# Loading block (0,1) of the adjacency matrix transposed at the start, holding it in four load buffers, and multiplying it in layer 0 in phase 1

## The reference

```python
# layer 0
adj_hat = adj + eye(N)
d = 1 / sqrt(sum(adj_hat, axis=1))
out = (adj_hat * d[:, None] * d[None, :]) @ (X @ W) + b
x = layernorm(x + relu(out))
# layer 1
support = x @ weight
output = relu(support + adj @ support + x @ self_weight)
x = layernorm(x + pair_norm(output))
```

## Time and profile before

| | |
|---|---|
| median of 3 runs | 1894.67 us (1894.28 to 1895.56) |
| profiled execution, its own time | 1894.09 us |
| its span in the trace | 1892.2 us |
| mean granted TensorE clock | 0.97 of full speed |
| TensorE, VectorE, ScalarE busy | 92%, 79%, 64% of the span |
| loaded | 566.49 MB from HBM, mean 302 GB/s |

### The profile page before, as it was taken

The page is one execution under the profiler, slowest core; times in us unless marked ns, Lnnn a source line. Parts: engine busy times, 40 slices in busy tenths (PEclk is TensorE's granted clock), DMA queues, the critical chain, the costliest instruction groups (busy, mean ns, idle before and its releaser), DMA issues.

```text
span 1892.2 us, 20585 instructions
## 1 busy us (share of the span) xinstructions
PE 1749.3 (92%) x7682; PEld 1416.7 (75%) x7682; DVE 1491.5 (79%) x1993; ACT 1208.4 (64%) x1648; POOL 21.5 (1%) x34
## 2 busy tenths in 40 slices
PE   2879998987999999989999999999989999999983
PEld 1657886866887888767788888888868888877862
DVE  4889788777878689986767575665589999999987
ACT  4576685785856646655555454454468888888865
POOL 0000000000000000100000000000000000000001
PEclk8999999999999999999999999999999999999995
DMA  9999999899998586954444455545589999999933
GB/s 397 421 422 421 417 399 421 332 397 402 374 384 362 199 355 280 352 181 154 160 174 178 178 178 189 189 176 186 194 322 386 386 386 386 386 376 369 384 149 89
DMA packets 80291, 572.03 MB, mean 302 GB/s; under 512 B 8960, under 2 KB 8960, under 8 KB 12096
## 3 DMA queue, kind: packets, MB, share of 16 engines
q1 hardware_dynamic: 76608, 557.88, 74.9%
q0 software_dynamic: 3584, 12.85, 2.2%
HBM read 566.49 MB, written 4.19 MB: 302 GB/s over the span
## 4 chain that ended last, share of the span: by engine, by line
PE 74%; DVE 15%; DMA 5%; ACT 4%; issue 2%; SPq 0%; POOL 0%; ACTq 0%; DVEq 0%
PE acc L1048 18%; PE acc L1050 18%; PE acc L1054 18%; PE pC L1030 4%; PE pD L1030 4%; DVE raw_low L731 4%; DMA s<-in_adjN 2%; DMA raw<-in_adjT 2%; DVE s L737 2%; ACT hi L557 1%; DVE o_low L731 1%; DVE zr_low L731 1%; DVE ux L810 1%; DMA zr<-in_adjT 1%; PE pA L1048 1%
## 5 line engine op out<-in xcount | busy, mean ns | idle before, releaser
L1048 PE MATMUL acc<-hi,rhi 128*128 128x512 f32 x1792 | 724.9, 405 | 76.6 <-DVE raw_low L731 23.7
L731 DVE TENSOR_TENSOR raw_low<-raw,hi 128x1024 fp32r<-128x1024 f32 x576 | 685.0, 1222 | 84.6 <-ACT hi L557 80.0
L557 ACT ACTIVATE hi<-raw 128x1024 fp32r<-128x1024 f32 x576 | 593.7, 1055 | 195.9 <-DMA raw<-in_adjT 68.7
L1054 PE MATMUL acc<-hi,rlo 128*128 128x512 f32 x1792 | 559.2, 394 | 0.0
L1050 PE MATMUL acc<-raw_low,rhi 128*128 128x512 f32 x1348 | 530.5, 394 | 0.0
L1048 PEld LDWEIGHTS acc<-hi,rhi 128*128 128x128 f32 x1792 | 341.2, 190 | 172.7 <-issue 34.7
L1054 PEld LDWEIGHTS acc<-hi,rlo 128*128 128x128 f32 x1792 | 340.8, 190 | 73.5
L1050 PEld LDWEIGHTS acc<-raw_low,rhi 128*128 128x128 f32 x1348 | 255.9, 190 | 54.8 <-issue 3.6
L731 DVE TENSOR_TENSOR zr_low<-zr,hi 128x1024 fp32r<-128x1024 f32 x148 | 177.8, 1223 | 29.0 <-ACT hi L557 26.6
L730 DVE TENSOR_TENSOR rlo<-zr,rhi 128x256 fp32r<-128x256 f32 x123 | 52.1, 424 | 177.3 <-ACT hi L557 177.1
L557 ACT ACTIVATE hi<-zr 128x1024 fp32r<-128x1024 f32 x148 | 155.3, 1060 | 57.0 <-PE pD L1030 19.1
(11 more groups left out here) (187 smaller groups left out, 1819.3 us busy)
## 6 DMA issues: line engine op xcount, KB each, us to landing
raw<-in_adjT SPq DMA_DIRECT2D x288, 1024.0 KB, 5.1
zr<-in_adjT SPq DMA_DIRECT2D x74, 1024.0 KB, 5.5
raw<-in_adjN SPq DMA_DIRECT2D x67, 1024.0 KB, 13.7
o<-in_adjT SPq DMA_DIRECT2D x32, 1024.0 KB, 11.0
s<-in_adjT SPq DMA_DIRECT2D x26, 1024.0 KB, 16.5
zr<-in_adjN SPq DMA_DIRECT2D x23, 1024.0 KB, 12.0
s<-in_adjN SPq DMA_DIRECT2D x22, 1024.0 KB, 12.4
s<-in_xT POOLq DMA_DIRECT2D x8, 512.0 KB, 7.3
```

Source lines behind the costliest of these rows:

```text
L557: S.activation(hi[n % DEEP][:, :], slice_of(chunk, j), ACT.Copy).then_inc(hi_ready, 1)
L731: V.tensor_sub(low_of(chunk, j), slice_of(chunk, j), hi[n % DEEP][:, :].bitcast(f32)).then_inc(slice_split, 1)
L1048: T.matmul(banks[h][:, :], a, hi[n % DEEP][:, part], start=opens, stop=False, skip_group_check=True)
L1054: last = T.matmul(banks[h][:, :], b, hi[n % DEEP][:, part], start=False, stop=end, skip_group_check=True)
```

## The change

Block (0,1) is no longer loaded as `adjN` in phase 1 and as `adjT` in phase 2. Its four chunks become a fourth kind, "hold": they are loaded transposed directly behind the first diagonal block, into the first four buffers. VectorE adds their eight slices to `colsum`, so that the block reaches row 0's degree with the diagonal's column sums. The buffers stay occupied until z of column block 1 is there; then the chunks are multiplied in layer 0 alone (units 4 and 5 of phase 1), not summed, and only then do their buffers go back into the queue. Block (0,1) leaves the dual visit of row 0 in phase 2, and its layer 1 part comes in phase 3, from a load of its own. The number of loads is 516 as before.

```diff
+    HELD = (0, 1)
...
         for c in range(k + 1, NB):
+            if (k, c) == HELD:
+                continue
             for q in qs:
                 sums.append(Chunk("sum", k, c, q, act=(q % 2 == 0 if k == 0 else (2 * c + q) % 4 != 3), stage=u))
         kept = [Chunk("keep", k, k, q, stage=u) for q in range(Q)] if qs[0] == 0 else []
         if u == 0:
-            chunks += kept + sums
+            hold = {q: Chunk("hold", *HELD, q, stage=u) for q in range(Q)}
+            chunks += kept + list(hold.values()) + sums
             continue
...
+            if i == by == HELD[1]:
+                v = new_visit(HELD[0], (L0,), 1)
+                products += [Chunk("mul", *HELD, q, layers=(L0,), visit=v, held=True, stage=u) for q in of]
...
     for k in (1, 0):
-        add_visit(k, (L0, L1), 2, list(range(NB - 1, k, -1)), final=True)
+        add_visit(k, (L0, L1), 2, [c for c in range(NB - 1, k, -1) if (k, c) != HELD], final=True)
...
+        if chunk.held:
+            chunk.buf, chunk.load = hold[chunk.q].buf, hold[chunk.q].load
+            free_buffers.append((chunk.buf, chunk.freed))
+            phase1_last[chunk.buf] = chunk.freed
+            continue
...
+        if chunk.kind == "hold":
+            continue
         free_buffers.append((chunk.buf, chunk.freed))
...
+        def col_steps(k):
+
+            return (k + 1) * (JB * Q - 1) + JB * Q
...
-                elif chunk.buf:
+                elif chunk.buf and not chunk.held:
...
-                k, q = chunk.row, chunk.q
+                k, q = chunk.row, chunk.q + (Q if chunk.kind == "hold" else 0)
...
-                pe.wait_ge(col_step, (k + 1) * (JB * Q - 1))
+                pe.wait_ge(col_step, col_steps(k))
```

More of the change, by code:

```diff
@@ L19 @@
     summed: bool = False
+    held: bool = False
     stage: int = -1
@@ L126, in graph_kernel @@
             products[n].tail = n - (len(products) - TAIL)
-        assert not kept or 2 * len(of) + TAIL <= len(products) - first
+        assert not kept or all(c.tail < 0 for c in products[first:] if c.row == k and c.summed)
         rest = TAIL if kept else TAIL - 3
@@ L136, in graph_kernel @@
             sums[at:at] = kept
-        room = ([1.0] * lead + [0.5 if k < NB - 2 else 1.0] * len(of) +
-                [1.0] * (len(products) - rest - first - len(of)))
+        stored = sum(1 for c in products[first:] if c.cached or c.held)
+        room = ([1.0] * lead + [0.5 if k < NB - 2 else 1.0] * stored +
+                [1.0] * (len(products) - rest - first - stored))
         share, put = len(sums) / sum(room), 0
@@ L749, in sum_kept @@
                 for j in range(JB):
-                    dve.wait_ge(col_step, k * (JB * Q - 1) + q * JB + j - 1)
+                    dve.wait_ge(col_step, (col_steps(k - 1) if k > 0 else 0) + q * JB + j - 1)
                     V.tensor_add(colsum, colsum, slice_of(chunk, j)).then_inc(col_step, 1)
@@ L768, in degree @@
                     dve.wait_ge(dve_summed, dve_sums_of[u])
-                    V.tensor_reduce(own[:, at], rsum[k % 2][:, (k + 1) * BG:].rearrange("p (c g) -> p g c", g=BG)[:, at],
+                    first = k + 2 if (k, k + 1) == HELD else k + 1
+                    V.tensor_reduce(own[:, at], rsum[k % 2][:, first * BG:].rearrange("p (c g) -> p g c", g=BG)[:, at],
                                     AX.X, ALU.add).then_inc(deg_step, 1)
@@ L937, in _ @@
                     continue
-                if chunk.kind == "keep":
+                if chunk.kind in ("keep", "hold"):
                     sum_kept(chunk)
```

## The result

The changed kernel takes 1903.62 us (median of 11 runs, 1899.61 to 1908.95) against 1895.56 us before (1893.34 to 1898.53, 11 runs): the ratio is 1.0042, with a 95% interval of 1.0033 to 1.0050. It is slower by 8.1 us. The forecast was 1898 us, 3.2 us slower, and gave "slower by over 3.8 us" the largest chance, 0.44. The profiled execution took 1900.17 us, 6.1 us more than that of before, and lies low among its runs; the runs of the changed kernel are spread over 9.3 us, those of before over 5.2 us.

The account below looks back on a forecast made before the run. Loads were taken to bound the kernel up to some 175 us, then mostly TensorE. 1894.09 + 10.9 - 21.6 + 10.9 + 3 = 1897.3 us, with 0.58 us for the median said as 1898 us; range 1888 to 1906 us.

Parts of the forecast that it names:

- Phase 2 loses 21.6 us: Phase 2, where TensorE never waits: four dual chunks of 5.40 us each fall away, 21.6 us less.
- Phase 3 gains 10.9 us: Phase 3: four single chunks of 2.72 us each are added, 10.9 us more, with their loads hidden.
- Phase 1 gains 10.9 us: Units 4 and 5 of phase 1: four unsummed chunks of 2.72 us add 10.9 us, charged in full.
- the three terms cancel: TensorE's products moved across phases 1, 2 and 3: 10.9 - 21.6 + 10.9 = +0.2 us.
- The late z of row 0: Start of the kernel: row 0's last sum comes 7.4 us later, but the work catches up by 175 us.
- rival C: Start: row 0's late z is not caught up by 175 us, shifting everything 7.4 us, to 1902 us; chance 0.10.
- What four buffers less cost: Loads until 230 us: 7 buffers in place of 11 stall the transfers, taken as +3 us.
- two releases of a buffer by TensorE: Loads at 126.78 and 156.14 us waited for TensorE; their buffers' next loads would be 0.8 and 2.8 us late.
- The upper bound, 10.3 us: Loads 25 to 67, slowed to phase 3's 386 GB/s: 43 x 0.24 = 10.3 us lost.
- The small things: Held chunks' high and low parts: 0.5 us a chunk, covered by the lead in `hi`; otherwise 2 us, in the range.
- Rival B: Load-bound stretch before 175 us: the queue runs shallow, 10.3 us lost in place of 3, giving 1905 us; chance 0.18.

Follow-up runs that it names:

- e1: Kernel before with only four buffers kept out of the rotation until units 4 and 5, leaving 7: 1906.52 us, ratio 1.0057.
- e3: Changed kernel with block (0,1) held but its layer 0 products left out, so it computes less: 1894.40 us, ratio 0.9991 to the kernel before.
- e6: Changed kernel with only chunks 0 and 1 held, until unit 7, multiplied near 403 us in one visit: 1898.96 us, ratio 1.0019 to before.
- e9: Changed kernel with only chunks 0 and 1 held, until unit 7, multiplied in a visit each: 1895.34 us, ratio 1.0000 to before.
- e2: Changed kernel with the new sums alone: the four buffers go back once summed, no product moved: 1895.51 us, ratio 1.0002 to before.
- e4: Kernel before with block (0,1)'s layer 0 products moved to phase 1's last unit, from four additional loads, one visit: 1899.15 us, ratio 1.0022.
- e10: Kernel before with block (0,1)'s layer 0 products moved to phase 1's last unit, from four additional loads, two visits: 1900.95 us, ratio 1.0027.
- e12: Changed kernel with three chunks of block (0,1) held, the fourth staying in phase 2's dual visit: 1898.87 us, ratio 1.0020 to before.
- e11: Kernel before with three buffers kept out of the rotation until units 4 and 5, leaving 8: 1897.08 us, ratio 1.0007.

## Why the prediction was right in its range and low in its size

The result lies inside the range of the forecast, 1888 to 1906 us, and on the side that had the largest chance; the sum behind it was 4.9 us too low (8.1 us slower against 3.2), and three of its four terms hold.

- **Phase 2 loses 21.6 us.** Measured 21.7. Right.
- **Phase 3 gains 10.9 us.** Measured 10.8. Right.
- **Phase 1 gains 10.9 us, none of it taken up by idle time.** Right within what the runs can tell. The 11.4 us between the first two marks are not the products alone, since e1 and e3, which have 7 buffers and no held products, also take 3.3 and 2.8 us more there than the kernel before. The cleaner comparison is the changed kernel against e3: 10.6 us between the degrees of rows 1 and 3, 9.2 us by the medians, so at most some 2 us were taken up. Even the longest idle time took none, by the marks of e6 (138.8 us against 132.9, for 5.4 us of products) and by e9's median. That products put into these waits moved everything behind fits the argument that the waits are tied to TensorE's own progress. So the three terms cancel, and the change has nothing to win.
- **The late z of row 0 costs nothing.** Right (e2), and rival C is out.
- **What four buffers less cost: "I take +3 us for both".** This is the step that failed. 7 buffers alone cost 10.8 us (e1), or 9.4 us by e3. The changed kernel's profiled execution shows 3.3 us of it up to the degree of row 1, and its median, 8.1 us over before, shows that this execution was a mild one. The step took two releases of a buffer by TensorE as the latest, and let the load of each be late once. The trace has five dips, the first near 80 us, which the two releases did not cover. The sentence "I stay near the lower end since six or seven buffers still keep more than two on their way" argues with an average, and the average holds (8 to 14 us to landing), but the queue runs nearly empty at moments, because SyncE waits in order for one buffer of a summed chunk and the next loads stand behind it. The upper bound, 10.3 us, was the right size by luck: it was worked out as an even slowing to 386 GB/s, and what happens is a full rate with dips to 302. Nor does that row of phase 3 show what two loads on their way can carry: TensorE is busy all the time there and takes a load each 2.72 us, which is 386 GB/s by itself.
- **The small things: "the lead of two chunks in `hi` covers".** It did not: the sum for VectorE left out the row sum beside the held chunks, and TensorE waits 2.2 us there. All waits up to the degree of row 2 together are 0.7 us longer than before (5.5 us against 4.8), and the range had 2 us for this.
- **Rival B (chance 0.18)** was thus nearest to the result, 1905 us, and C at 1902 us came as near by its number although its mechanism is out. The forecast's own range, 1895 to 1901 us, missed the median by 2.6 us.

The prediction weighed the single 1 MB transfer at 341 GB/s of the Trainium skill, "DMA: Bandwidth & Descriptors", section Bandwidth, with an estimate of 26 us. With 7 buffers the loss was 10.8 us, and between dips the rate is some 420 GB/s with three to six loads on their way. The page's figure, which it gives for transfers issued from GpSimd, is not tested by that: no run here has its loads, issued by SyncE, one at a time at full demand.

What stays open: 2.5 us of the profiled execution's difference lie between the degrees of rows 2 and 3. e4 and e10, which are the program of before there, take 3.4 and 2.3 us more than it in that stretch, so this is no more than scatter. e12 keeps 3.5 us, of which its 8 buffers explain at most the 1.4 us of e11, and the wait of 2.2 us behind the held chunks was not taken out by itself. Whether the changed kernel (8.1 us, interval 6.3 to 9.5) really loses less than e1 (10.8 us, 8.5 to 13.3) can't be told, since the intervals overlap. No version tried beats the kernel before; the best, e9, equals it.

## What to carry to other kernels

Moving work between two stretches that the same engine bounds wins nothing, however idle that engine looks somewhere else: ask first whether its idle time is set by its own progress, which an experiment that puts the work there shows at once. Buffers held for long are paid in steps, not in shares: here two of eleven cost nothing, three no more than 3 us and four 10.8 us, so a price for them needs the worst moment of the rotation and not its mean depth. When an edit changes how many visits rotate through a few accumulators, look at the place where the rotation meets the next stage: between e6 and e9 one visit made 3 us far away from the edit.

## What the runs showed of the hardware that I had not expected

A load stream recovers from a dip at once: outside its seven slices of 302 to 371 GB/s the changed kernel's transfers run at 409 to 432 GB/s (most near 420) with three to six loads on their way (8 to 14 us to landing at 2.5 us a load), the same rate as with some eight before. With four to six (10 to 14 us in e12) every slice between 46 and 175 us stays at 412 GB/s or more, so a shorter queue lost nothing here until it ran nearly empty. The runs of the changed kernel also scatter more, 9.3 us between the fastest and the slowest of 11 against 5.2 us before; e3, with the same buffers held, has 5.6 us, so the thin rotation alone does not explain that.
